# Moves inside the second layer's sixteen slots: keys, turned sums, turned x, first queries and values, picking, reciprocals and scatters

## The reference

```
x = x + tanh(g_xattn[0]) * attention0(layernorm(x), ctx)          # 16 heads of 16
x = x + tanh(g_ffn[0])   * recurrent0(layernorm(x))               # gates with a carried state
x = x + tanh(g_xattn[1]) * attention1(layernorm(x), ctx)          # 16 heads of 64
x = x + tanh(g_ffn[1])   * experts1(layernorm(x))                 # shared expert + 8 best of 64

def attention1(q, kv):                     # per sequence and head
    scores = (q @ Wq) (kv @ Wk)^T / 8      # 112 x 375
    out = softmax(scores) @ (kv @ Wv)      # 112 x 64
    return concat(out) @ Wo + bo

def experts1(x):                           # per row
    aff = x @ centroids.T;  idx = top_k(aff + expert_biases, 8)
    w = sigmoid(aff[idx]);  w = w / (sum(w) + 1e-8)
    return silu(x @ Ws_up) @ Ws_down + sum_k w_k * silu(x @ W_up[idx_k]) @ W_down[idx_k]
```

## Time and profile before

| | |
|---|---|
| median of 3 runs | 2482.11 us (2477.03 to 2484.4) |
| the profiled execution's own time | 2478.53 us |
| its span, first to last instruction | 2476.8 us |
| PE busy | 2375.4 us, 96% |
| DVE busy | 1608.7 us, 65% |
| ACT busy | 1583.1 us, 64% |
| POOL busy | 728.8 us, 29% |
| mean granted TensorE clock | 0.984 |

### The profile page before, as it was taken

One profiled execution on the slowest core, in us unless ns is written; L12 is line 12 of the kernel. 1 busy time (PEld: TensorE's weight loads), 2 busy tenths in 40 slices (PEclk: granted clock), 3 DMA queues, 4 the chain that ended last, 5 costly groups with the idle time before them and its releaser, 6 DMA issues. The chain is left out here.

```text
span 2476.8 us, 63160 instructions
## 1 busy us (share of the span) xinstructions
PE 2375.4 (96%) x19886; PEld 1804.3 (73%) x19887; DVE 1608.7 (65%) x5036; ACT 1583.1 (64%) x4814; POOL 728.8 (29%) x870
## 2 busy tenths in 40 slices
PE   7999999999998999999999999999999969999996
PEld 5788778778776566666666666666766648888885
DVE  4777777777774466776776767766667763333338
ACT  2777777777774566666666665665665637777770
POOL 2000000000000023233232232332332346777771
PEclk8999999999999999999999999999999989999999
DMA  5111111111111411111111111111111166776679
GB/s 160 39 44 47 45 42 47 45 42 47 47 35 36 137 30 43 34 43 43 37 43 39 40 43 35 44 43 31 49 41 32 38 181 194 215 218 209 208 265 381
DMA packets 145298, 210.14 MB, mean 85 GB/s; under 512 B 23977, under 2 KB 108507, under 8 KB 145027
## 3 DMA queue, kind: packets, MB, share of 16 engines
q1 hardware_dynamic: 114322, 139.92, 18.8%
q0 software_dynamic: 26544, 60.21, 7.3%
q10 hardware_dynamic: 4160, 6.55, 0.7%
HBM read 118.21 MB, written 96.75 MB: 87 GB/s over the span
## 5 line engine op out<-in xcount | busy, mean ns | idle before, releaser
L1456 ACT ACTIVATE wup<-bank,nmax 112x375 f32<-112x375 f32 x512 | 296.7, 585 | 110.7 <-DVE nmax L1564 109.5
L767 ACT ACTIVATE prob<-bank,nmax 112x375 f32<-112x375 f32 x512 | 291.5, 578 | 66.6 <-DVE nmax L845 62.5
L845 DVE TENSOR_REDUCE nmax<-bank 112x1 f32<-112x375 f32 x512 | 254.9, 539 | 68.7 <-PE bank L589 68.7
L1909 POOL DMA_INDIRECT expert_rows<-rows,ids x248 | 237.2, 957 | 154.2 <-ACT wup L1456 107.2
L1564 DVE TENSOR_REDUCE nmax<-bank 112x1 f32<-112x375 f32 x512 | 255.3, 541 | 20.3 <-PE bank L1252 20.1
L1315 PE MATMUL bank<-wup,wk 128*128 128x375 f32 x512 | 219.9, 512 | 2.2 <-DMA wup<-context_turned 1.0
L1021 POOL TENSOR_TENSOR stats<-stats,neg_half 112x1 f32<-112x1 f32 x64 | 35.1, 549 | 618.0 <-DVE stats L875 613.9
L1462 ACT COPY pT<-bank 128x336 f32<-128x336 f32 x512 | 201.4, 451 | 19.2 <-PE bank L1259 18.9
L1876 POOL TENSOR_TENSOR stats<-stats,neg_half 112x1 f32<-112x1 f32 x64 | 35.7, 557 | 564.9 <-DVE stats L1595 562.6
L596 PE MATMUL bank<-ident,prob 112*128 112x112 f32 x1536 | 197.2, 263 | 2.7 <-ACT prob L767 1.3
L1252 PE MATMUL bank<-wup 64*112 64x375 f32 x1024 | 194.6, 498 | 3.3 <-ACT wup L1456 3.3
(11 more groups left out here) (284 smaller groups left out, 5280.0 us busy)
## 6 DMA issues: line engine op xcount, KB each, us to landing
xr<-expert_rows SPq DMA_DIRECT2D x274, 129.0 KB
wup<-expert_results SPq DMA_DIRECT2D x14, 1024.0 KB, 17.9
wdn<-expert_results SPq DMA_DIRECT2D x14, 1024.0 KB, 20.6
wdn<-in_L_ffn_W_down_dram SPq DMA_DIRECT2D x8, 1024.0 KB, 12.4
expert_rows<-nowhere SPq DMA_DIRECT2D x56, 129.0 KB, 2.8
x_and_h_in<-stage SPq DMA_DIRECT2D x32, 224.0 KB, 2.5
xt<-x_and_h_in SPq DMA_DIRECT2D x32, 224.0 KB, 2.8
context_turned<-ctxT SPq DMA_DIRECT2D x32, 187.5 KB, 2.2
```

Of the source, the lines that this page charges most:

```text
L767: nc.scalar.activation(prob[:, n % RING, :NK], s_bank[r][:NQ, :NK], ACT.Exp, bias=nmax[:, r:r + 1], accum_out=rsum[:, par, h:h + 1]).then_ ...
L845: nc.vector.tensor_reduce(nmax[:, r:r + 1], s_bank[r][:NQ, :NK], AX, ALU.max, negate=True).then_inc(maxed, 1)
L1456: nc.scalar.activation(prob[:, n % RING, :NK], s_bank[r][:NQ, :NK], ACT.Exp, bias=nmax[:, r:r + 1], accum_out=rsum[:, par, n:n + 1]).then_ ...
L1909: nc.gpsimd.indirect_dma_start(rows_d, bass.IndirectOffsetOnAxis(ap=ids[:, k:k + 1], axis=0), rows[:, k, :], None).then_inc(scattered, 16)
```

## The change

The change touches only numbers: the slots of entries in `ORDER_C`, the slots of the small DVE steps in `parts_y` and `inverses`, and the thresholds in `spaced`. No instruction is added or dropped, no lane changes, no buffer changes, and the DMAs are the same.

```
 ORDER_C = [
-    (1, "post", "va3", "dve"), (1, "own", "v10", "act"), (1, "own", "v11", "dve"),
-    (2, "own", "r0", "act"), (2, "post", "wo", "dve"), (3, "own", "v12", "act"), (3, "pre", "k2", "dve"),
-    (5, "pre", "k4", "act"), (5, "post", "lnT", "dve"), (6, "pre", "k1", "act"), (6, "pre", "xT", "dve"),
+    (1, "post", "va3", "dve"), (1, "own", "v10", "act"), (1, "own", "v11", "dve"), (2, "own", "v12", "act"),
+    (2, "post", "wo", "dve"), (2, "own", "r0", "act"), (3, "pre", "xT", "dve"), (4, "pre", "k4", "act"),
+    (5, "post", "lnT", "dve"), (5, "pre", "k1", "act"), (6, "pre", "k2", "dve"), (7, "own", "r1", "act"),
     (7, "own", "va0", "dve"), (8, "pre", "k0", "act"), (8, "post", "router", "dve"), (9, "post", "shared_up", "act"),
-    (9, "pre", "k3", "dve"), (9, "own", "r1", "act"), (10, "pre", "k5", "act"), (10, "own", "va1", "dve"),
-    (10, "own", "r2", "act"), (12, "pre", "q0", "act"), (12, "pre", "v00", "dve"), (12, "pre", "v01", "act"),
+    (9, "pre", "k3", "dve"), (9, "own", "r2", "act"), (10, "pre", "k5", "act"), (10, "own", "va1", "dve"),
+    (11, "pre", "q0", "act"), (11, "pre", "v00", "dve"), (11, "pre", "v01", "act"), (13, "post", "rank", "dve"),
...
-                parts_y = [(2, moments_y), (4, norm_y), (9, choose), (11, sigmoids), (12, weigh), (9, shared_silu),
-                           (15, lambda p: pick(p, range(0, 2))), (14, lambda p: pick(p, range(2, 6))),
-                           (13, lambda p: pick(p, range(6, 8))), (15, place_end)]
+                parts_y = [(2, moments_y), (4, norm_y), (9, shared_silu), (10, choose), (10, sigmoids),
+                           (12, weigh), (14, lambda p: pick(p, range(2, 6))), (14, lambda p: pick(p, range(6, 8))), (15, lambda p: pick(p, range(0, 2))), (15, place_end)]
...
-                    for v, at in enumerate((0, 7, 8, 12)):
+                    for v, at in enumerate((2, 4, 7, 12)):
...
-                    pool.wait_ge(exped, H * (p + 2) + 6 + 5 * k // 4)
+                    pool.wait_ge(exped, H * (p + 2) + 7 + 4 * k // 4)
```

More of the change, by code:

```diff
@@ L34 @@
 ORDER_C = [
-    (1, "post", "va3", "dve"), (1, "own", "v10", "act"), (1, "own", "v11", "dve"),
-    (2, "own", "r0", "act"), (2, "post", "wo", "dve"), (3, "own", "v12", "act"), (3, "pre", "k2", "dve"),
-    (5, "pre", "k4", "act"), (5, "post", "lnT", "dve"), (6, "pre", "k1", "act"), (6, "pre", "xT", "dve"),
+    (1, "post", "va3", "dve"), (1, "own", "v10", "act"), (1, "own", "v11", "dve"), (2, "own", "v12", "act"),
+    (2, "post", "wo", "dve"), (2, "own", "r0", "act"), (3, "pre", "xT", "dve"), (4, "pre", "k4", "act"),
+    (5, "post", "lnT", "dve"), (5, "pre", "k1", "act"), (6, "pre", "k2", "dve"), (7, "own", "r1", "act"),
     (7, "own", "va0", "dve"), (8, "pre", "k0", "act"), (8, "post", "router", "dve"), (9, "post", "shared_up", "act"),
-    (9, "pre", "k3", "dve"), (9, "own", "r1", "act"), (10, "pre", "k5", "act"), (10, "own", "va1", "dve"),
-    (10, "own", "r2", "act"), (12, "pre", "q0", "act"), (12, "pre", "v00", "dve"), (12, "pre", "v01", "act"),
-    (13, "post", "rank", "dve"), (13, "own", "r3", "act"), (14, "post", "shared_down", "dve"),
-    (14, "pre", "v02", "act"), (15, "pre", "k6", "dve"), (15, "pre", "q1", "act"), (15, "own", "va2", "dve"),
-    (15, "pre", "k7", "act"),
+    (9, "pre", "k3", "dve"), (9, "own", "r2", "act"), (10, "pre", "k5", "act"), (10, "own", "va1", "dve"),
+    (11, "pre", "q0", "act"), (11, "pre", "v00", "dve"), (11, "pre", "v01", "act"), (13, "post", "rank", "dve"),
+    (13, "own", "r3", "act"), (14, "post", "shared_down", "dve"), (14, "pre", "v02", "act"), (15, "pre", "k6", "dve"),
+    (15, "pre", "q1", "act"), (15, "own", "va2", "dve"), (15, "pre", "k7", "act"),
 ]
```

## The result

| | before | after |
|---|---|---|
| median (20 runs each) | 2481.66 us (2476.71 to 2484.4) | 2483.93 us (2481.02 to 2487.09) |
| ratio | | 1.0014, 95% interval 1.0008 to 1.002 |
| span of the profiled execution | 2476.8 us | 2479.3 us |
| PE / DVE / ACT busy | 2375.4 / 1608.7 / 1583.1 us | 2370.6 / 1577.9 / 1571.8 us |

The time hardly moved: it rose by 2.3 us, and the interval of the ratio lies just above 1. Both profiled executions ran some 3 us under their medians (2478.53 and 2481.02). The traces show that the small rise is the sum of two larger numbers of opposite sign. I cut both spans at the same events of PE: the first of the 20 idle transposes at the layer's start, the first scores, the first `wo` (slot 2 of sequence 1), the thirty-first, the last, the end.

What follows compares the result with a forecast made beforehand. PE, busy 96% of the span, was taken as the bound. +0.03 a sequence gave +1 us over 30, fixed costs +5.0, in all +6 on the median 2482.1: 2488 us, range 2477 to 2499.

Steps and rivals of the forecast that it cites:

- the disputed term: Second scores behind `wo`: with `r0` moved behind `wo`, PE waits for head 7's exponential, +0.2 us a sequence.
- the third rival: Whole kernel: gains and wait cancel, later waits take the three fixed costs back, 2482 to 2485 us; chance 0.08.
- What the move of v12 ahead of wo frees: PE at `r0` and ahead of `va0`: waits for the `v11` and `xT` copies go, 0.18 and 0.09, together -0.27 a sequence.
- What the move of r0 behind wo costs: PE after `wo`: second scores wait for ACT's `r0` copy and two exponentials, starting 1.97 after `wo`; +0.2 a sequence.
- r1 in slot 7: ACT's `r1` copy ahead of `k0`: an even race, 3.4 us on ACT and PE; +0.05 a sequence, from 0 to 0.2.
- New neighbours: `lnT` behind scores, `k1` and `k4` behind transposes: distances change by +0.05 a sequence, from -0.1 to +0.15.
- On PE nothing moves: First queries and values: ACT's copies of `q0` and `v01` move ahead of turned copies, needed over 2 us later; 0.
- The head: Start of the layer: `xT` stands first and waits for `norm_x`, so `k0` comes later, +2.4 us once.
- The last sequence: No keys to fill there: turns of heads 0 and 1 to second scores take 6.37 instead of 5.46, +0.9 us.
- Reciprocals at nothing: DVE reciprocals in new slots: PE does not wait for them, 0; the fourth's 1.88 spreading copy should be free.
- The slow rival: ACT's string comes later than counted, second scores wait 0.3 more: +0.33 a sequence, 2497 us; chance 0.27.
- the fast one: Second scores do not wait and keys run shorter: -0.4 a sequence, `wo` to `wo` 37.2, 2475 us; chance 0.15.

Runs made afterwards that it cites:

- run 3: The changed kernel with ACT taking the exponentials of heads 6 and 7 before it copies `r0`: median 2478.90 us, ratio 0.9988.
- run 5: The kernel before with only `v12` ahead of `wo`, `r0` behind it and the first reciprocal in slot 2: 2494.45 us, one run.
- run 6: The changed kernel with `r1` back in slot 9, `r2` in slot 10 and their reciprocals in slots 7 and 8: 2487.67 us, one run.
- run 2: The changed kernel with 56 instead of 20 idle transposes ahead of the first `xT`: 2485.09 us, one time.
- run 9: The changed kernel with the first reciprocal back in slot 0 for sequence 0 alone: 2481.89 us, one run.
- run 1: The changed kernel with the old order of entries only at the head of the layer: median 2480.61 us, ratio 0.9999.
- run 4: The changed kernel with `choose` back in slot 9 ahead of `shared_silu`: 2484.68 us, one time.
- run 10: The kernel before with only `r1` moved to slot 7, `r2` to slot 9 and their reciprocals to slots 4 and 7: 2488.18 us, one run.

## Why the prediction was right, and where its steps were wrong

The forecast was 2488 us and no clear change; it came out at 2483.93. The mechanism of the disputed term stood, but two sums were off in opposite directions: the once-only stretches cost 8.4 us instead of 5, and the 30 sequences gained 6.4 us where a loss of 1 was forecast. That the total came so near is luck. The time also lies in the numbers of the third rival (2482 to 2485), but not for its reason: no later wait took the fixed costs back.

- *"What the move of v12 ahead of wo frees"*, -0.27: half right. The 0.18 at `r0` went. The 0.09 ahead of `va0` was no wait for the copy of `xT`: it left the turns and came back behind `r1`, +0.09. What made the sum right even so (-0.18 and -0.09) is a term that it lacks, by luck of the same size: the uncovered weight load of `wo`.
- *"What the move of r0 behind wo costs"*, +0.2: right in mechanism, time and place (1.91 against 1.97 after `wo`). The key ahead of these scores takes 0.92, where it took 0.73 before; run 3 got back 0.18. Run 5 confirmed the string by a second fill.
- *"r1 in slot 7"*, +0.05: right that it is even for PE: `k0` is followed after 0.74 before and after, and 0.74 without `r1` there. But what `r1` covers (the copy of `k2`) was not seen, 0.14 by run 6.
- *"New neighbours"*, +0.05: `xT` and `lnT` +0.08, the three keys -0.12 without the wait (2.04 instead of 2.15, with the 0.18 of run 3 taken off). Wrong sign, within its stated bounds.
- *"On PE nothing moves"* for first queries: the step that failed most plainly. Before, `q0` stood next behind `r2` on the same lane and waited for ACT's copy; its group took 1.88, not 1.79. This and the 0.05 of `r2` were missing, with 0.03 given back at the turns between. Together: -0.25 a sequence instead of +0.03, 7.5 us over 30; the longer sequences took 1.8 of it back, where the kernel before had 0.6.
- *The head*, +2.4: it measured +5.4, more than twice that. The wait alone was 2.4 to 2.8, as forecast, and the clock behind it 2.6 more (run 2), a term that the sum did not have.
- *Sequence 0*, +1.7, measured +1.70, its cause shown by run 9. *The last sequence*, +0.9: from the turns of heads 0 and 1 to the second scores 6.24 against 5.46 before, +0.8 of the +1.2; the rest was not traced.
- *Reciprocals at nothing*: right for PE in the steady part, and no spreading copy of 1.88 stands in the usual sequence. But POOL's row copy now met another DVE step, the masked one, in some sequences, and the fourth spreading copy in others. The prediction asked to look for such meetings, but feared them at the second spreading copy and held the stretch of the fourth to be free.
- The slow rival's condition (+0.33 by ACT's string) did not come; the fast one's distance of 37.2 nearly did (37.32), though by other terms: the scores do wait.

## What to carry to other kernels

When a list of steps also runs once as a prologue, price the prologue apart: there little work stands ahead of a wait to cover it, and an idle PE may pay a second time through its clock. A wait that just ends in time on a shared bank still costs an uncovered weight load, so look for such waits by comparing distances of the same group at different places. Before pricing a longer distance as a wait, look for the same neighbours at a place where nothing waits: `va0` is 0.09 late there too. And before undoing or keeping half of a reordering, try both halves alone: here they are worth 0 and +0.31 apart, and -0.25 together.

## What the runs showed of the hardware

- Behind 4.42 us of an idle PE the granted clock was 0.50 for about 6.8 us; with 56 transposes in that time it stayed at 1.00. Behind the stand of 2.36 us in sequence 0 it fell for 3.4 us in nine of 13 traces (not in runs 1, 3, 4 and 10), and behind the stand of 3.03 there for 3.4 us in runs 3 and 4 and 6.8 us in run 5, not in four others that have it. Code that is the same at that place pays or doesn't pay 1.6 us, and no edit here decides which.
- Behind the waits for `v11`'s and `r2`'s copies the first weights were loaded at the start of their matmul and not ahead of it, and the group was 0.09 us longer (`wo` 3.54 and 3.45; `q0` 1.88 in the four traces in which `r2` stands behind `va1`, 1.79 in the other nine). A late load alone doesn't show a wait: the weights of `va0` are loaded at its start in the last sequence too, where it waits for nothing.
- An instruction of 0.22 us on DVE became 1.97 beside a row copy of POOL that started 0.01 us earlier; started 0.01 later, POOL's took 1.97 instead of 1.90. A spreading copy of 0.29 that came while the row copy ran took 0.51 to 0.80 in the changed kernel.
